# A fused two-layer kernel: copies, products and gate operations moved behind the scan's own work, and the scan's first rows of dt and B made by TensorE

## What is computed

```
L0: x = x + ga * attention(layernorm(x)*(1+ca)+sa)     4 heads, dilations 1, 2, 4, 8
    x = x + gb * ffn(layernorm(x)*(1+cb)+sb)           input and weight quantised in blocks of 32 to a 6-bit grid
L1: x = x + ga * mamba(layernorm(x)*(1+ca)+sa)
    x = x + gb * recurrent(layernorm(x)*(1+cb)+sb)

mamba:  x_branch, z = split(x @ in_proj)               512 channels each
        x_branch = silu(causal conv of 4 taps + bias)
        B (16), C (16), dt (1) = x_branch @ x_proj
        dt = softplus(dt * dt_proj_w + dt_proj_b)      per channel and time
        h  = exp(dt*A) * h + dt * B * x_branch         16 states per channel
        y  = sum over states of h*C, + D*x_branch;  y * silu(z) @ c_proj
recurrent: c = sigmoid(.)*c + sigmoid(.)*tanh(.)       over the 4 sequences, 1024 rows at a time
        tanh(x @ wo + c @ uo + bo)
```

## Time and profile before

| | |
|---|---|
| median of 3 runs | 1267.78 us (1267.23 to 1269.12) |
| the profiled execution | 1265.77 us |
| its span, first to last instruction | 1264.5 us |
| mean granted TensorE clock | 0.986 |
| PE busy | 1140.8 us (90%) |
| DVE busy | 1155.2 us (91%) |
| ACT busy | 795.0 us (63%) |
| POOL busy | 982.6 us (78%) |

### The profile page before, as it was taken

One profiled execution on the slowest core, in us unless ns is written; L12 is line 12 of the kernel. 1 busy time (PEld: TensorE's weight loads), 2 busy tenths in 40 slices (PEclk: granted clock), 3 DMA queues, 4 the chain that ended last, 5 costly groups with the idle time before them and its releaser, 6 DMA issues.

```text
span 1264.5 us, 12574 instructions
## 1 busy us (share of the span) xinstructions
PE 1140.8 (90%) x3612; PEld 640.1 (51%) x3612; DVE 1155.2 (91%) x1138; ACT 795.0 (63%) x1445; POOL 982.6 (78%) x712
## 2 busy tenths in 40 slices
PE   7989678998999899997999899997999899789996
PEld 5636333664457444764457443763457443444453
DVE  3768999999999999899999999899999999999987
ACT  2256567765786668755786668755786667655532
POOL 3216886889778887989778997889778996976862
PEclk9999989999999999999999999999999999899998
DMA  7308588766868688866878679876868786899922
GB/s 285 115 16 315 176 269 284 278 233 233 281 226 297 200 278 292 289 233 225 290 219 301 197 277 311 276 241 217 292 217 287 215 282 236 290 335 346 374 86 116
DMA packets 92309, 313.87 MB, mean 248 GB/s; under 512 B 10432, under 2 KB 15680, under 8 KB 91984
## 3 DMA queue, kind: packets, MB, share of 16 engines
q1 hardware_dynamic: 89936, 306.26, 70.3%
q10 hardware_dynamic: 2304, 6.82, 1.5%
HBM read 301.73 MB, written 11.31 MB: 248 GB/s over the span
## 4 chain that ended last, share of the span: by engine, by line
PE 43%; DVE 22%; POOL 14%; ACT 9%; issue 8%; DMA 3%; SPq 0%; DVEq 0%; POOLq 0%; ACTq 0%
PE ps L907 13%; DVE ps L1741 12%; POOL arena L1970 8%; PE ps L601 5%; PE ps L830 4%; PE ps L609 3%; DVE arena L1749 3%; DMA arena<-bc_scratch 2%; PE ps L647 2%; PE ps L751 2%; PE ps L723 2%; ACT ps L1295 2%; ACT arena L931 2%; PE ps L728 1%; PE ps L633 1%
## 5 line engine op out<-in xcount | busy, mean ns | idle before, releaser
L1970 POOL TENSOR_TENSOR arena<-arena 128x1024 f32<-128x1024 f32 x255 | 600.3, 2362 | 136.5 <-PE ps L907 113.2
L1741 DVE TENSOR_TENSOR_SCAN ps<-ps,arena 128x1024 f32<-128x1024 f32 (+1 forms) x257 | 585.8, 2280 | 30.3 <-ACT ps L1295 17.9
L907 PE MATMUL ps<-arena,identF 128*128 128x512 f32 x1024 | 482.8, 603 | 49.0 <-DVE arena L1749 29.4
L1295 ACT ACTIVATE ps<-arena,negA 128x512 f32<-128x512 f32 x512 | 332.7, 683 | 83.2 <-DVE arena L1749 78.2
L907 PEld LDWEIGHTS ps<-arena,identF 128*128 128x128 f32 x1024 | 190.3, 193 | 267.2 <-issue 208.8
L1749 DVE TENSOR_TENSOR arena<-ps,arena 128x1024 f32<-128x1024 f32 (+1 forms) x257 | 312.0, 1214 | 5.9
L922 ACT ACTIVATE arena<-arena,rnln 128x256 f32<-128x256 f32 x118 | 61.9, 589 | 42.1 <-POOL rnln L1776 24.9
L647 PE MATMUL ps<-arena,inw 128*128 128x512 f32 x128 | 60.0, 614 | 11.7 <-ACT arena L931 9.6
L1307 ACT ACTIVATE arena<-ps 128x2 f32<-128x2 f32 x128 | 22.0, 172 | 64.9 <-DVE arena L1749 64.4
L931 ACT ACTIVATE arena<-ps,modT 128x512 f32<-128x512 f32 x43 | 51.7, 1266 | 14.7 <-PE ps L474 12.6
L728 PE MATMUL ps<-arena,inw 128*128 128x512 f32 x128 | 60.2, 592 | 0.0
(11 more groups left out here) (222 smaller groups left out, 1707.1 us busy)
## 6 DMA issues: line engine op xcount, KB each, us to landing
arena<-bc_scratch SPq DMA_DIRECT2D x511, 512.0 KB, 5.0
arena<-in_x SPq DMA_DIRECT2D x16, 256.0 KB, 6.9
arena<-in_x SPq DMA_DIRECT2D x8, 512.0 KB, 8.4
xr_scratch<-arena SPq DMA_DIRECT2D x6, 512.0 KB, 6.9
px_scratch<-arena SPq DMA_DIRECT2D x6, 512.0 KB, 6.1
out_x<-arena SPq DMA_DIRECT2D x5, 512.0 KB, 2.6
arena<-bc_scratch SPq DMA_DIRECT2D x9, 256.0 KB, 3.6
woT<-in_woT SPq DMA_DIRECT2D x4, 512.0 KB, 10.0
```

Source lines behind the costliest of these rows:

```text
L907: x = pe.matmul(ps[:, Y, :], identF[:], inp[:, m % RING, q, :], start=False, stop=(i == BLOCK_STEPS - 1 and q == 1), skip_group_check=True)
L1295: x = act.activation(ps[:, 2 * (m % 2) + q, :], dt[:, kd, :], ACT.Exp, scale=negA[:, kd, 2 * i + q:2 * i + q + 1])
L1741: x = dve.tensor_tensor_scan(states, states, inp[:, m % RING, q, :].rearrange("p q t -> p (q t)"), 0.0, ALU.mult, ALU.add)
L1970: x = pool.tensor_tensor(inp[:, m % RING, :, :], u[:, kd:kd + 1, :].broadcast_to([P, 2, TH]), b_at[:, m % 3, :, :], ALU.mult)
```

## The change

At the start: the replicated weights and their products (`dtw_rep`) go. Once `bc_sb` is in SBUF, TensorE picks single rows of it with a column of the identity matrix and spreads them over 128 partitions in PSUM (`pe_row`): the row of dt, then the first two rows of B. The softplus is made in two pairs, the second at step 10.5 from a dt row made anew at step 10.25. VectorE makes `hB1` ahead of u and takes the first B rows from PSUM. GpSimd's u for the second pair moves from step 6 to 11.75. TensorE's transposes for the second half stand in `pe_first`. SyncE no longer fetches B rows for step 0, and fetches C's for step 0 in that place.

In the table: `k1` and the second `cp_ev` move by a quarter past ScalarE's scan part, `v0` past TensorE's, `i_g` and `c_new` past one and two of GpSimd's products (not for g = 6), and `gb_bias` of the second half from 16.25 to 19.5, behind `q_back`.

```diff
-  "pe_before": ... "v0": 5.25,
+  "pe_before": ... "v0": 6,
-  "act_before": ... "k1": 4.25,
+  "act_before": ... "k1": 4.5,
-  "act_after": {"cp_ev": (2.75, 5), ...
+  "act_after": {"cp_ev": (2.75, 5.25), ...
-  "pool_second": ... "gb_bias": 16.25,
+  "pool_second": ... "gb_bias": 19.5,
-  "pool_after": {... "i_g": 25.5, "c_new": 25.5},
+  "pool_after": {... "i_g": 26.25, "c_new": 27.25},

 # sp_scan
-            if quarter == 0 and 0 <= m < G * STEPS:
+            if quarter == 0 and 1 <= m < G * STEPS:
...
-                    sp.dma_start(b_at[:, 0, 0, :], bc_d[0, 0:1, :].broadcast_to([P, TH])).then_inc(S.first_row, 16)
-                    sp.dma_start(b_at[:, 0, 1, :], bc_d[0, 1:2, :].broadcast_to([P, TH])).then_inc(brow_in[0], 16)
+                    sp.dma_start(c_at[:, 0, :, :], bc_d[0:1, NS:NS + 2, :].broadcast_to([P, 2, TH])).then_inc(crow_in[0], 16)

 # pe_first
-            pe.wait_ge(S.halved, 2)
...
-            for p in (0, 2):
-                for kd in (p, p + 1):
-                    pe.wait_ge(S.xc, kd + 1)
-                    x = pe.matmul(ps[0:2 * NS + 1, 0, :], xpw[:, kd, :], xc[:, kd, :], start=(kd == 0), stop=(kd == KD - 1))
-                if p:
-                    x.then_inc(S.bc_mm, 1)
-                for kd in (p, p + 1):
-                    x = pe.matmul(ps[:, 1, :], dtw_rep[:, kd, :], xc[:, kd, :], start=(kd == 0), stop=(kd == KD - 1))
-            x.then_inc(S.dt_mm, 1)
+            for kd in range(KD):
+                pe.wait_ge(S.xc, kd + 1)
+                x = pe.matmul(ps[0:2 * NS + 1, 0, :], xpw[:, kd, :], xc[:, kd, :], start=(kd == 0), stop=(kd == KD - 1))
+            x.then_inc(S.bc_mm, 1)
+            pe.wait_ge(ln["ln1"].hn, 4)
+            for k in range(KE):
+                pe_transposes(hn1, k, X0 + k, ln["ln1"].mm)
+            pe.wait_ge(S.bc_sb, 1)
+            pe_row(2 * NS, 1).then_inc(S.dt_mm, 1)
+            for q in range(2):
+                pe_row(q, 2 + q).then_inc(S.first_row, 1)
+            yield 10.25
+            pe.wait_ge(S.z_ev, 4)
+            pe_row(2 * NS, Y0).then_inc(S.dt_mm, 1)
+
+        def pe_row(row, bank):
+            return pe.matmul(ps[:, bank, :], identF[0:2 * NS + 1, row:row + 1].broadcast_to([2 * NS + 1, P]), bc_sb, start=True, stop=True)

 # act_first
             act.wait_ge(S.dt_mm, 1)
-            for kd in range(KD):
-                x = act_softplus(kd, dt[:, kd, :], ps[:, 1, :])
...
+            act_softplus(0, dt[:, 0, :], ps[:, 1, :]).then_inc(S.sp_first, 1)
+            act_softplus(1, dt[:, 1, :], ps[:, 1, :]).then_inc(S.softplus, 1)
             act_table(ACT.Exp, 2)
+            yield 10.5
+            act.wait_ge(S.dt_mm, 2)
+            for kd in (2, 3):
+                x = act_softplus(kd, dt[:, kd, :], ps[:, Y0, :])
+            x.then_inc(S.softplus, 1)

 # dve_first
-            dve.wait_ge(S.sp_first, 1)
-            dve.tensor_tensor(u[:, 0, :], dt[:, 0, :], xc[:, 0, :], ALU.mult).then_inc(S.first_dt, 1)
             for k in range(KE):
                 dve.wait_ge(ln["ln1"].mm, 3 + k)
                 dve_ln_cols("ln1", hB1, X0 + k, k, 0, 0, True)
+            dve.wait_ge(S.sp_first, 1)
+            dve.tensor_tensor(u[:, 0, :], dt[:, 0, :], xc[:, 0, :], ALU.mult).then_inc(S.first_dt, 1)
             dve.wait_ge(S.first_dt, 1)
             for q in range(2):
-                dve.wait_ge(brow_in[0] if q else S.first_row, 16)
-                x = dve.tensor_tensor(inp[:, 0, q, :], u[:, 0, :], b_at[:, 0, q, :], ALU.mult)
+                dve.wait_ge(S.first_row, q + 1)
+                x = dve.tensor_tensor(inp[:, 0, q, :], u[:, 0, :], ps[:, 2 + q, :], ALU.mult)

 # pool_first
-            pool.tensor_copy(dtw_rep, xpw[:, :, 2 * NS:2 * NS + 1].broadcast_to([P, KD, P])).then_inc(S.halved, 1)
...
-            yield 6
+            yield 11.75
             pool.wait_ge(S.softplus, 2)
+            pool.wait_ge(S.first_dt, 2)
```

More of the change, by code:

```diff
@@ L66 @@
         "softplus": (33.75, 33.75), "dt_copy": 41.25, "xc_silu": 28.5},
-    "act_after": {"cp_ev": (2.75, 5), "z_tanh": (5.75, 8, 8.5, 9.25), "hA": (10.25, 10.25),
+    "act_after": {"cp_ev": (2.75, 5.25), "z_tanh": (5.75, 8, 8.5, 9.25), "hA": (10.25, 10.25),
         "gate": (12.25, 15.75, 17.5, 20.25, 22.5, 26), "sigmoid": (11.5, 17.5, 17, 21.5, 22.5, 25.25),
@@ L80 @@
     "pool_second": {"ln1_rstd": -10.25, "ga_bias": -7.5, "op_add": (11.75, 11.75), "ln2_rstd": 13, "n2a": 13.5,
-        "n2b": 13.5, "q_scale": 16.25, "gb_bias": 16.25, "q_sub": 17.75, "q_back": 17.75, "ffn_add": (20.25, 20.25),
+        "n2b": 13.5, "q_scale": 16.25, "gb_bias": 19.5, "q_sub": 17.75, "q_back": 17.75, "ffn_add": (20.25, 20.25),
         "ln3_rstd": 22.75, "u": (34.5, 39.25), "cut": (34.5, 42)},
-    "pool_after": {"cp_gate": -7.25, "cp_add": (5, 5), "ln4_rstd": 6.75, "f_c": 21, "i_g": 25.5, "c_new": 25.5},
+    "pool_after": {"cp_gate": -7.25, "cp_add": (5, 5), "ln4_rstd": 6.75, "f_c": 21, "i_g": 26.25, "c_new": 27.25},
 }
@@ L653, in pe_before @@
             T = TIMES["pe_second" if h == 1 else "pe_before"]
-            yield t + T["hn1_t0"]
-            pe.wait_ge(S.bc_sb, h)
-            pe.wait_ge(ln["ln1"].hn, 2 * h + 2)
-            pe_transposes(hn1, 0, X0, ln["ln1"].mm)
-            yield t + T["hn1_t1"]
-            pe.wait_ge(S.xc, 4 * h)
-            pe_transposes(hn1, 1, X1, ln["ln1"].mm)
+            if h > 1:
+                yield t + T["hn1_t0"]
+                pe.wait_ge(S.bc_sb, h)
+                pe.wait_ge(ln["ln1"].hn, 2 * h + 2)
+                pe_transposes(hn1, 0, X0, ln["ln1"].mm)
+                yield t + T["hn1_t1"]
+                pe.wait_ge(S.xc, 4 * h)
+                pe_transposes(hn1, 1, X1, ln["ln1"].mm)
             yield t + T["q0"]
@@ L989, in act_first @@
             act.wait_ge(S.dt_mm, 1)
-            for kd in range(KD):
-                x = act_softplus(kd, dt[:, kd, :], ps[:, 1, :])
-                if kd == 0:
-                    x.then_inc(S.sp_first, 1)
-                elif kd % 2:
-                    x.then_inc(S.softplus, 1)
-            act_table(ACT.Exp, 2)
+            act_softplus(0, dt[:, 0, :], ps[:, 1, :]).then_inc(S.sp_first, 1)
+            act_softplus(1, dt[:, 1, :], ps[:, 1, :]).then_inc(S.softplus, 1)
+            act_table(ACT.Exp, 2)
+            yield 10.5
[3 more added lines that the diff above has]
+            x.then_inc(S.softplus, 1)
         def act_table(func, n):
@@ L1286, in act_decay @@
                 act.wait_ge(S.bc_sb, 1)
-                act.wait_ge(S.softplus, 2)
+                act.wait_ge(S.softplus, 1)
             elif m == 1:
@@ L1873, in pool_before @@
             pool.tensor_tensor(src, src, per_block(qinv, nblk), ALU.mult).then_inc(S.q_step, 1)
-            yield t + T["gb_bias"]
-            pool_bias_to_residual(GB0, 1, 2 * h + 2, xrow)
+            if h > 1:
+                yield t + T["gb_bias"]
+                pool_bias_to_residual(GB0, 1, 2 * h + 2, xrow)
             yield t + T["q_sub"]
@@ L1881, in pool_before @@
             pool.tensor_tensor(out, out, per_block(qsc, nblk), ALU.mult).then_inc(S.q_step, 1)
+            if h == 1:
+                yield t + T["gb_bias"]
+                pool_bias_to_residual(GB0, 1, 2 * h + 2, xrow)
             for q in range(2):
@@ L1925, in pool_after @@
             pool.tensor_tensor(gates["f"], gates["f"], c_of(g), ALU.mult).then_inc(S.c_f, 1)
-            yield t + TIMES["pool_after"]["i_g"]
+            yield t + (25.5 if g == G - 2 else TIMES["pool_after"]["i_g"])
             pool.wait_ge(S.g_sig, 2 * g + 2)
@@ L1929, in pool_after @@
             pool.tensor_tensor(gates["i"], gates["i"], gates["c"], ALU.mult).then_inc(S.i_g, 1)
-            yield t + TIMES["pool_after"]["c_new"]
+            yield t + (25.5 if g == G - 2 else TIMES["pool_after"]["c_new"])
             pool.wait_ge(S.c_f, g + 1)
@@ L1966, in pool_scan @@
                 pool.wait_ge(S.u, 2 * h + kd // 2 + 1)
-            pool.wait_ge(brow_in[m % 3], 16 * (m // 3 + 1))
+            pool.wait_ge(brow_in[m % 3], 16 * (m // 3 + (m % 3 > 0)))
             if m >= RING:
```

3 lines of the change are left out of this document (1 added, 2 removed), and 2 rows, old and new, of the table TIMES.

## The result

| kernel | median | runs | lowest to highest |
|---|---|---|---|
| before | 1268.51 us | 6 | 1267.23 to 1270.34 |
| after | 1275.88 us | 6 | 1274.33 to 1276.67 |

The ratio is 1.0056 (95% interval 1.0043 to 1.0068): the change makes the kernel 7.1 us slower (5.5 to 8.6). I had forecast 1269.8, which was 2.1 over the 1267.78 known then, with 1274.5 as the upper end. The profiled execution of the kernel after took 1276.37 us (span 1274.8, mean granted clock 0.978; before 1265.77, 1264.5 and 0.986).

A forecast was written before the change was run, and what follows sets the result against it. No single engine was taken as the bound: TensorE sets the pace in the attention part, VectorE's scan elsewhere. Terms -2.9 + 0.8 + 2.4 + 0 + 1.8 = +2.1 us gave 1269.8, range 1263.5 to 1274.5.

The forecast's parts named there:

- the start: Up to the first scores: dt and B rows by TensorE bring scores 3.9 us earlier; 2.9 kept after the first half's loss.
- the late i\*g and c in the even halves: g = 0, 2, 4: GpSimd idles, then lags; TensorE waits for step 127's products and loses 0.8 each, 2.4 us in all.
- g = 5: Half without attention: products lag, scans 222 to 226 come later, and 1.8 us stay lost (0.5 to 2.5).
- g = 1 and 3: Halves without the added carry: products need less time, the accumulation is reached just in time, loss 0 (to 1).
- Accumulation of step 31 ahead of v0 in half 2: TensorE waits for step 31's products ahead of v0 and loses 0.8 us.
- the falling clock: Rival at the start: TensorE's clock falls after k0, or B's transfer is late; start gives 1.0 only, 1271.8; chance 0.12.
- The give-back: First half: moved bias and u product delay the additions of ffn and VectorE's statistics; loss 1.0 us (0.5 to 1.6).
- The softplus pair, the table loads and the u product: Near steps 10 to 12: late softpluses and table loads hide in ScalarE's idle time, u in GpSimd's wait; cost nothing.
- GpSimd's lag is the bound: Rival: lag lasts to the statistics, scan 134 late, halves lose 1.8 each; +8.7, 1276.5; chance 0.13.

The follow-up runs named there:

- ic_even2: Kernel before with i*g and c moved in g = 0, 2 and 4 alone: 1273.01 us, ratio 1.0032.
- ic_only: Kernel before with only i*g and c moved: 1273.81 us, ratio 1.0044.
- ic_odd: Kernel before with i*g and c moved in g = 1 and 3 alone: 1268.84 us, ratio 1.0004.
- ic_five2: Kernel before with i*g and c moved at g = 5 alone: 1268.35 us, ratio 0.9997.
- ic_back: Kernel after with only i*g and c put back to their old places: 1268.84 us, ratio 0.9997.
- start_only: Kernel after with all four reorders undone (v0, k1's copy, the projection's copy, i*g and c): 1267.97 us, ratio 0.9993.
- reorder_only: Kernel before with the four reorders alone (v0, k1's copy, the projection's copy, i*g and c): 1275.83 us, ratio 1.0066.
- ic_back_fill: ic_back with matmuls filling both TensorE gaps, as in fill: 1268.33 us, ratio 0.9999.
- start_fill: start_only with matmuls filling both TensorE gaps, as in fill: 1267.93 us, ratio 0.9989.
- start_u1: start_only with VectorE's u product for the second group of channels moved ahead of scan 0: 1268.44 us, ratio 0.9997.
- start_adds: start_only with GpSimd's bias a product earlier and the additions of ffn's output ahead of product 16: 1269.78 us, ratio 1.0010.
- v0_back: Kernel after with only TensorE's v0 put back ahead of the accumulation of step 31: 1272.27 us, ratio 1.0033.
- start_gatefill: start_only with only the two filler matmuls ahead of the first gate product: 1268.13 us, ratio 0.9992.
- fill: Kernel after with extra matmuls in two TensorE gaps (steps 40 and 43 of a half, g = 0 to 5): 1274.26 us, ratio 1.0046.

## Why the prediction was wrong, step by step

The forecast was +2.1, the result +7.1. The steps that failed are sizes of terms: the start was put at -2.9 and gave -0.9, the late i\*g and c in the even halves were put at 2.4 and cost 4.1, and TensorE's clock had no term at all outside the start. The term for g = 5 failed the other way.

- **i\*g and c in the even halves (2.4 forecast).** Mechanism right, term mis-sized: 4.1 by ic_even2, 0.9 to 1.1 for each half by the steps, against 0.8. I had the loss come from TensorE's new order. It doesn't need it: ic_only has the old order and loses 0.9 at each.
- **g = 1 and 3 (0).** Right: ic_odd, and 0.1 to 0.5 for each half by the steps.
- **g = 5 (1.8).** Wrong: ic_five2 is not slower. I took my times from one execution, in which the output gate had run in a dip (3.64 at 1075.28, where ic_only has 2.24), and claimed that nothing behind the lag gives the time back. With such a dip that is nearly what happens (1.5). Without it the wait for the decay of scan 222, which is there anyway, takes the lag in. A dip stands around this place in 11 of the 16 profiles, so some loss should still show in the times of ic_five2. That it doesn't is not explained.
- **Accumulation of step 31 ahead of v0 in half 2 (0.8).** Right in place and size by the steps: TensorE waited 0.78 at 241.16, and C-products 34 to 38 lost 0.8. In the times the three small reorders together cost 0.5 by the ratios without the late i\*g and c (ic_back less start_only, 0.9 by the medians) and 2.8 with them (reorder_only less ic_only); the first is not clear of nothing.
- **Start (-3.9, 1.0 back, so -2.9).** Measured with the reorders undone: 0.9 faster (by the ratio's interval 2.0 faster to 0.3 slower). The lead of 3.9 exists where q0 runs at full clock (4.4 at step 14 in ic_back, 3.9 in ic_back_fill, 3.7 in start_fill) and is 2.0 to 2.4 where q0 meets the lower clock, as in start_only, start_u1, start_adds, v0_back and start_gatefill. I had counted on full speed because TensorE no longer idles ahead of q0, and gave the falling clock 0.12. In the profiled executions of the kernel after and of fill the clock stayed up and the locked product took the 2.1 instead, which left 2.2 and 2.1 at step 14. The give-back by step 20 was 1.1 to 1.7, against 1.0, dips between 150 and 200 us included; VectorE's statistics waited the forecast 0.8 for GpSimd in start_only. The softplus pair, the table loads and the u product cost nothing, as forecast: the lead is the same at steps 6 and 14. Three of the four table loads were followed at once by the activation that needed them; ahead of the fourth's activation ScalarE waited 0.32 for TensorE's row.
- **No term for the clock elsewhere.** By the steps of the profiles 4.8 of the 10.2. But the profile of the kernel before was a lucky one: 1265.77 us, faster than every one of the 98 runs of it in these comparisons, whose median is 1269.0. So about 3 of the 10.2 are that choice of baseline, and the medians, not the two profiles, are what the terms must add to.

The sum by the measured parts, all by ratios: start -0.9, odd halves +0.5, even halves +4.1, g = 5 -0.4, small reorders +0.5: +3.8, where the change measured +7.1. By fewer and larger parts it closes: start_only -0.9 and reorder_only +8.4 make +7.5. Between the two lie ic_only, 5.6 where its three parts add to 4.2, and the small reorders, 2.8 beside the late i\*g and c where they are 0.5 without. The parts' intervals are about 1 to 2 each way, so it is not shown that the parts act on each other; by the steps 0.6 of it is there, the 0.2 more in each even half.

**What stays open** is whether late i\*g and c also bring more dips. For it: of the six profiles with both moves late in the even halves four have two or three dips between 280 and 1070 us (after, v0_back, reorder_only, ic_only), one has one (ic_even2) and one none (fill); of the ten others nine have none or one, and ic_odd two. The mean granted clock is 0.9792 in the kernel after against 0.9808 in ic_back. Against it: v0_back has 0.9809 with the late moves and start_only 0.9807 without them. And fill and ic_back_fill, with the dips at the seams gone in both, still stand 5.9 apart. Their profiles stand 7.1 apart: 3.9 at the moved operations, 1.2 at a dip at 1144, and 2.0 ahead of step 32, from the locked product at the start of fill and a longer dip at 216. The 98 runs of the kernel before have mean clocks from 0.978 to 0.986: a dip is a matter of the single execution, so one profile for each kernel can't settle it.

Of the rivals, "GpSimd's lag is the bound" gave 1276.5, close to the result, but not by its mechanism: by the steps halves lost 0.1 to 1.1, not 1.8, and scans 70 and 134, where it was to show, waited for nothing in the kernel after. Its nearness is luck.

## What to carry to other kernels

An operation that fills the time in which a strictly ordered engine can't do its main work is in the right place, even where others seem to wait for what it delays: moved behind that work, it becomes lag for all its consumers, and reordering them only moved the wait here (0.85 at v0, 0.79 for a copy, 0.68 at the projection). A term read from one execution holds for that execution: at g = 5 the same move cost 1.5 or 0.1, by whether TensorE's clock had dipped just before. A profile of one execution can be several microseconds off the kernel's median; before a plan is made from a difference between two profiles, subtract the stretches where the granted clock differs, and set terms against medians.

## What the runs showed of the hardware

- The same TensorE work behind the same gap of 1.36 us runs at either level of the clock: four instructions in 1.98 or in 3.65. The four such stretches in the kernel after that the kernel before lacks cost 1.0 to 1.7 us of the end each. One at 1075 to 1078 (the kernel before, ic_odd) cost nothing by itself.
- Matmuls that fill the gaps kept the clock up (mean 0.9792 to 0.9828 in fill, 0.9807 to 0.9843 in start_fill), and by the times they gave 1.6 us or nothing, neither clear of nothing.
- One VectorE product with two inputs in SBUF took 2.78, 0.92, 0.87 and 0.69 us in four kernels. Begun while a GpSimd product ran it ended 0.55 after that one's end (2.78, 0.92, 0.87), and it held up the next GpSimd product (2.80 to 2.84 for 2.37).
